# Selective scan of a fused Mamba-2 decoder layer: rows of cumulated time steps spread over the partitions by DMA instead of by TensorE

## What is computed

```python
zxbcdt = x @ w_in.T                       # z 512, xs 128, B 128, C 512, dt 4
xBC = silu(causal_conv4(xBC) + conv_b)
dt = softplus(dt + dt_bias); a = dt * -exp(A_log)
cs = cumsum(a, axis=time)                 # per sequence and head
Ldec = where(t >= s, exp(cs[t] - cs[s]), 0)
att = (C @ B.T) * Ldec
Y = att @ (xs * dt) + D * xs
y = Y * silu(z); out = y @ w_out.T
```

## Time and profile before

| | |
|---|---|
| median of 3 runs | 413.46 us |
| span of the profiled execution, first to last instruction | 411.9 us |
| the profiled execution's own time | not listed apart; the span is 1.6 us under the median |
| TensorE busy | 398.4 us, 97% of the span, 1936 matmuls |
| VectorE busy | 288.8 us, 70% |
| ScalarE busy | 189.7 us, 46% |
| POOL busy | 130.2 us, 32% |
| chain that ended last | TensorE 82%, VectorE 11%, ScalarE 3% |
| DMA | 25.52 MB in 11659 packets |

### The profile page before, as it was taken

The page is one execution under the profiler, slowest core; times in us unless marked ns, Lnnn a source line. Parts: engine busy times, 40 slices in busy tenths (PEclk is TensorE's granted clock), DMA queues, the critical chain, the costliest instruction groups (busy, mean ns, idle before and its releaser), DMA issues.

```text
span 411.9 us, 5385 instructions
## 1 busy us (share of the span) xinstructions
PE 398.4 (97%) x1936; PEld 318.3 (77%) x1936; DVE 288.8 (70%) x517; ACT 189.7 (46%) x383; POOL 130.2 (32%) x117
## 2 busy tenths in 40 slices
PE   7999999999999989999999999999999999999984
PEld 3878887766669987888888888887788788787753
DVE  3596991146886669888897989695567656675676
ACT  6768745736555564343425252863314133142131
POOL 3504215614524553565654737740000000000000
PEclk8999999999999999999999999999999999999999
DMA  7901111010000106111112131352110120110002
GB/s 248 316 2 52 53 51 51 2 51 2 0 1 2 52 2 204 53 51 53 51 51 60 44 99 49 113 179 74 51 53 25 52 78 25 51 54 22 28 0 77
DMA packets 11659, 25.52 MB, mean 62 GB/s; under 512 B 1681, under 2 KB 1809, under 8 KB 11634
## 3 DMA queue, kind: packets, MB, share of 16 engines
q1 hardware_dynamic: 10482, 23.10, 17.1%
q10 hardware_dynamic: 1152, 2.10, 1.4%
HBM read 23.10 MB, written 2.10 MB: 61 GB/s over the span
## 4 chain that ended last, share of the span: by engine, by line
PE 82%; DVE 11%; ACT 3%; issue 1%; DMA 1%; SPq 0%; ACTq 0%; DVEq 0%
PE bank L582 23%; PE bank L584 23%; PE bank L583 23%; PE bank L653 2%; PE bank L640 2%; PE bank L847 2%; PE bank L858 1%; DVE sets_f L1491 1%; DMA rows<-x 1%; PE bank L869 1%; PE bank L621 1%; DVE tmp L1668 1%; PE bank L662 1%; DVE big L1459 1%; PE bank L829 1%
## 5 line engine op out<-in xcount | busy, mean ns | idle before, releaser
L582 PE MATMUL bank<-sets,station 128*128 128x512 f32 (+1 forms) x424 | 164.1, 387 | 1.8 <-DVE station L1539 1.2
L584 PE MATMUL bank<-sets,station 128*128 128x512 f32 (+1 forms) x424 | 158.5, 374 | 0.0
L583 PE MATMUL bank<-sets,station 128*128 128x512 f32 (+1 forms) x424 | 158.3, 373 | 0.0
L582 PEld LDWEIGHTS bank<-sets,station 128*128 128x128 f32 x424 | 80.0, 189 | 19.5 <-issue 3.6
L583 PEld LDWEIGHTS bank<-sets,station 128*128 128x128 f32 x424 | 79.9, 189 | 15.4 <-issue 2.2
L584 PEld LDWEIGHTS bank<-sets,station 128*128 128x128 f32 x424 | 79.8, 188 | 14.3
L540 POOL TENSOR_TENSOR big<-tmp,side_f 128x512 f32<-128x512 f32 x17 | 26.4, 1569 | 24.0 <-DVE side_f L1555 24.0
L1425 DVE SCALAR_TENSOR_TENSOR big<-bank,cw,big 128x508 f32<-128x508 f32 (+2 forms) x36 | 26.2, 739 | 5.1 <-ACT big L1026 4.2
L462 POOL TENSOR_TENSOR station<-raw,station 128x1024 fp32r<-128x1024 f32 x7 | 16.8, 2395 | 40.2 <-ACT station L968 40.2
L1269 ACT ACTIVATE small<-small 128x1 f32<-128x1 f32 x24 | 7.0, 294 | 47.9 <-DVE small L1670 47.9
L1555 DVE TENSOR_TENSOR side_f<-side_f,bank 128x512 f32<-128x512 f32 x36 | 24.5, 684 | 4.1 <-PE bank L584 3.8
(11 more groups left out here) (182 smaller groups left out, 670.8 us busy)
## 6 DMA issues: line engine op xcount, KB each, us to landing
raw<-wstream SPq DMA_DIRECT2D x31, 512.0 KB, 3.4
rows<-x SPq DMA_DIRECT2D x8, 256.0 KB, 5.0
big<-ctxT SPq DMA_DIRECT2D x8, 256.0 KB, 2.6
big<-ctx SPq DMA_DIRECT2D x8, 256.0 KB, 2.9
out<-tmp ACTq DMA_DIRECT2D x8, 256.0 KB, 2.0
big<-ln_w SPq DMA_DIRECT2D x1, 256.0 KB, 5.4
big<-lora_b SPq DMA_DIRECT2D x3, 64.0 KB, 5.2
ga<-gate_lora SPq DMA_DIRECT2D x1, 72.0 KB, 5.3
```

Source lines behind the costliest of these rows:

```text
L582: pe.matmul(ps, a_hi, b_lo, start=first, stop=False)
L583: pe.matmul(ps, a_hi, b_hi, start=False, stop=False)
L584: return pe.matmul(ps, a_lo, b_hi, start=False, stop=last)
```

## The change

Row h of the running sums is copied by DMA from its one partition to all 128, four DMAs of 256 KB for each half (`spread_decays`), into `decays`, which holds 4 heads x 512 tokens a half. VectorE adds the mask once for each half (`mask_decays`), ScalarE takes the exponential in place, and att, skip and y_of work on that buffer. The five matmuls (L638, L640) go. The dt rows are computed twice, in partitions 0 to 3 and 32 to 35, with a multiplier of 1 for the second set, so that one 128x128 turn of `steps` gives both columns. time_steps of both halves moves up to behind conv_taps(3). The first half's buffer is in the memory of set T2, which is written again by the turned tiles later.

```diff
-N_TAPS = 4
-DT_LO = 32
+N_TAPS = 5
+DT_ROW = 32
+DT_LO = 2 * DT_ROW
+STEP_ROWS = DT_ROW + H
...
-        dec = big[:, 10752:11776].rearrange("p (b h q) -> p b h q", b=2, h=H)
-        negcs = big[0:H, 11776:12800]
...
+        decays = (at("decays0", SETS_AT + T2 * 2 * CH, [P, 2 * CH])[:, :], big[:, 10752:12800])
...
+        future = big[:, 13056:13184]
...
-        dt_row = tmp[0:H, 2048:3072]
-        sel = tmp[0:H, 3072:3584].rearrange("p (h q) -> p h q", h=H)
+        steps = tmp[:, 2048:3072]
+        negcs = steps[0:STEP_ROWS, :]
+        dt_row = sets[0:STEP_ROWS, T3, 0, :, :].rearrange("p c n -> p (c n)")
...
+        def dec(b):
+
+            return decays[b // HB].rearrange("p (h t) -> p h t", h=H)[:, :, bass.ts(b % HB, L)]
...
-            for dst, src in ((alog[:, :], a_log), (dtb[:, :], dt_bias), (cw[:, :, :], conv_w), (cb[:, :], conv_b)):
+            sp.wait_ge(small_set, 1)
+            for dst, src in ((alog, a_log), (dtb[0:H, :], dt_bias), (dtb[DT_ROW:STEP_ROWS, :], dt_bias),
+                             (cw[:, :, :], conv_w), (cb[:, :], conv_b)):
...
+            def spread_decays(hf):
+
+                sp.wait_ge(cs_ok, HB * (hf + 1))
+                for h in range(H):
+                    sp.dma_start(decays[hf][:, bass.ts(h, HALF)],
+                                 steps[h:h + 1, half(hf)].unsqueeze(1).broadcast_to([1, P, HALF])) \
+                        .then_inc(decays_in[hf], 16)
+
             for n in range(RAW, LOOP_CHUNK):
                 sp.wait_ge(w_lo, n - RAW + 1)
                 load_chunk(n)
+                if n == RAW + 2:
+                    spread_decays(0)
+                    spread_decays(1)
...
+            pool.memset(steps, 0.0).then_inc(pool_setup, 1)
...
+                    w_dt, lo_dt = blocks(ringS[:, 0, 0, 0:D]), blocks(ringS[:, 0, 1, 0:D])
+                    pool.tensor_copy(w_dt[:, :, DT_LO:DT_LO + H], lo_dt[:, :, 0:H].bitcast(F32)).then_inc(dt_lo, 1)
+                    pool.tensor_copy(w_dt[:, :, DT_LO + DT_ROW:DT_LO + STEP_ROWS], lo_dt[:, :, 0:H].bitcast(F32)) \
+                        .then_inc(dt_lo, 1)
+                    pool.tensor_copy(w_dt[:, :, DT_ROW:STEP_ROWS], w_dt[:, :, 0:H].bitcast(F32)).then_inc(dt_lo, 1)
...
                 pe.wait_ge(cs_ok, b + 1)
-                if b >= 2:
-                    pe.wait_ge(dec_exp, H * (b - 1))
-                if b == 0:
-                    pe.wait_ge(pool_setup, 8)
-                pe.matmul(bank[b % 2][:, :], identb[:, :], future, start=True, stop=False)
-                for h in range(H):
-                    pe.matmul(bank[b % 2][:, bass.ts(h, L)], sel[:, h, :], negcs[:, tok(b)],
-                              start=False, stop=(h == H - 1))
...
-                pe.transpose(bank[5][:, P:P + H], negcs[:, tok(b)], ident[0:H, 0:H])
-                pe.transpose(bank[5][:, P + H:P + 2 * H], dt_row[:, tok(b)], ident[0:H, 0:H])
+                pe.transpose(bank[5][:, P:2 * P], steps[:, tok(b)], ident[:, :])
...
-                act.activation(xb[:, b % 2, :], bank[5][:, 0:P + 2 * H], ACT.Copy).then_inc(xb_ok, 1)
+                act.activation(xb[:, b % 2, :], bank[5][:, 0:P + STEP_ROWS], ACT.Copy).then_inc(xb_ok, 1)
                 act.wait_ge(xb_ok, b + 1)
+                act.wait_ge(masked, b // HB + 1)
                 for h in range(H):
 
-                    act.activation(dec[:, b % 2, h, :], bank[b % 2][:, bass.ts(h, L)], ACT.Exp,
+                    act.activation(dec(b)[:, h, :], dec(b)[:, h, :], ACT.Exp,
...
+            v.memset(small[0:STEP_ROWS, 2:5], 1.0).then_inc(small_set, 1)
...
-                if i == 4:
+                if i == 3:
                     softplus_relu(1)
-            time_steps(0)
-            v.wait_ge(pool_setup, 8)
+                    time_steps(0)
+                    time_steps(1)
+
+            def mask_decays(hf):
+
+                d = decays[hf].rearrange("p (k q) -> p k q", q=L)
+                v.wait_ge(decays_in[hf], 16 * H)
+                v.tensor_tensor(d, d, future.unsqueeze(1).broadcast_to([P, HB * H, L]), ALU.add).then_inc(masked, 1)
+
+            v.wait_ge(pool_setup, 6)
+            mask_decays(0)
             v.wait_ge(const_in, 16 * N_CONST)
             for h in range(H):
                 mm = v.tensor_scalar(dI[:, h, :], ident[:, :], dsk[:, h:h + 1], None, ALU.mult)
             mm.then_inc(vec_setup, 1)
-            time_steps(1)
+            mask_decays(1)
```

More of the change, by code:

```diff
@@ L222, in build @@
         dsk = small[:, 5:5 + H]
-        dtb = small[0:H, 2:3]
+        dtb = small[0:STEP_ROWS, 2:3]
         alog = small[0:H, 3:4]
-        expa = small[0:H, 4:5]
+        expa = small[0:STEP_ROWS, 4:5]
         ga = sb("ga", [P, DC, E + E * RANK])
@@ L262, in build @@
         dt_ok, a_ok, cs_ok = sem("dt_ok"), sem("a_ok"), sem("cs_ok")
+        small_set = sem("small_set")
+        decays_in = [sem(f"decays_in{i}") for i in range(2)]
+        masked = sem("masked")
         cv_init, cv_tap, cv_done = sem("cv_init"), sem("cv_tap"), sem("cv_done")
@@ L444, in _ @@
             pool.memset(ident[:, :], 0.0).then_inc(pool_setup, 1)
-            pool.memset(sel, 1.0).then_inc(pool_setup, 1)
+            pool.memset(future, 0.0).then_inc(pool_setup, 1)
             pool.wait_ge(pool_setup, 2)
@@ L448, in _ @@
                                base=0, pattern=[[-1, P]], channel_multiplier=1).then_inc(pool_setup, 1)
[L449 to L453, removed]
             pool.affine_select(out=future, in_=future, compare_op=ALU.is_ge, fill=FUTURE, base=0,
-                               pattern=[[0, H], [1, L]], channel_multiplier=-1).then_inc(pool_setup, 1)
+                               pattern=[[1, L]], channel_multiplier=-1).then_inc(pool_setup, 1)
+            pool.memset(steps, 0.0).then_inc(pool_setup, 1)
             for e in range(E):
@@ L661, in y_of @@
                     pe.wait_ge(z_done, 6)
-                pe.matmul(bank[7][:, :], xb[:, b % 2, 0:P], dec[:, b % 2, :, :], start=True, stop=True) \
+                pe.matmul(bank[7][:, :], xb[:, b % 2, 0:P], dec(b), start=True, stop=True) \
                     .then_inc(y_ps, 1)
@@ L1006, in softplus_rest @@
                 act.wait_ge(ip_done, n + 1)
-                act.activation(dt_row[:, half(hf)], bank[IN_BANK[n]][DT_LO:DT_LO + H, :], ACT.Copy).then_inc(sp_rest, 1)
+                act.activation(dt_row[:, half(hf)], bank[IN_BANK[n]][DT_LO:DT_LO + STEP_ROWS, :], ACT.Copy) \
+                    .then_inc(sp_rest, 1)
             def softplus_abs(hf):
@@ L1392, in softplus_sum @@
                 v.wait_ge(sp_rest, hf + 1)
-                v.tensor_tensor(dt_row[:, half(hf)], bank[IN_BANK[n]][0:H, :], dt_row[:, half(hf)], ALU.add) \
+                v.tensor_tensor(dt_row[:, half(hf)], bank[IN_BANK[n]][0:STEP_ROWS, :], dt_row[:, half(hf)], ALU.add) \
                     .then_inc(sp_sum, 1)
@@ L1457, in att @@
                 for h in range(H):
[L1459 to L1461 removed]
+                    v.scalar_tensor_tensor(out=dec(b)[:, h, :], in0=bank[6][:, bass.ts(h, L)],
+                                           scalar=xb[:, b % 2, P + DT_ROW + h:P + DT_ROW + h + 1],
+                                           in1=dec(b)[:, h, :], op0=ALU.mult, op1=ALU.mult).then_inc(att_ok, 1)
             def gate_y(b):
```

25 lines of the change are left out of this document (9 added, 16 removed).

## The result

The changed kernel took 460.76 us, the median of 4 runs (460.22 to 462.54), beside 413.50 us for the kernel before (4 runs, 413.33 to 414.28). The ratio is 1.1138, 95% interval 1.1116 to 1.1160: slower by 47.3 us. The forecast was 407.0; what happened is rival 1, which had 463, and the sign that the prediction named for being wrong is there: TensorE waits at tile 1's product for VectorE, whose mask waits for a DMA.

The account below looks back on a forecast made before the run. The prediction took TensorE, busy 68.5 of 69 us, to bound the scan, with VectorE and ScalarE cutting the gain: of 11.0 us removed 6.5 remain, other parts cost nothing, so 413.46 - 6.5 = 407.0 us; range 404 to 466.

Parts of the forecast that it names:

- rival 1: Spread DMAs: rows leave their partition one at a time, tile 1's product 51.3 us late; 463 us, chance 0.27.
- the sign that the prediction named for being wrong: At tile 1's product: TensorE waits for VectorE, whose mask waits for a DMA; no size given.
- Part 4: The eight 256 KB DMAs from one SBUF row each: landed by 47 us, needed by about 66.8 us.
- its two ends: Time of the eight DMAs: 5.2 us at 401 GB/s, or 83.6 us at one engine's 25.1 GB/s.
- Part 3: POOL, start and SP's queue: extra casts, memset and loads cost nothing, at most 0.3 us; no load starts later.
- Part 1: TensorE in the scan: 1.38 us less per tile, 11.0 for eight, of which 6.5 us reaches the end.
- some 0.03 us: Chain of tiles 0 to 4: added cost each of the larger xb copy and the exponential reading SBUF.
- The sum of 6.5 us: Scan: gain of 6.20 by tile 4's scores, some 0.6 more behind att(4), 0.3 taken off for small additions.
- the forecast's own case: Whole kernel: fast DMAs and part of TensorE's gain kept, 407.0 us, own range 402.4 to 411, chance 0.50.
- Part 2: VectorE: time_steps moved behind conv_taps(3) cost nothing, at worst 1 us; two masks of 2.3 us each are hidden.
- The sentence that warned of POOL for the masks: VectorE's masks: beside a reading POOL a small operation went from 0.41 to 1.49 us, but POOL is free then.
- the two slower rivals: Spread DMAs: one row at a time, 463 us, chance 0.27; two streams at a time, 421 us, chance 0.15.

Follow-up runs that it names:

- Experiment 1: Kernel before plus extra 256 KB DMAs into unused memory, single, then paired on two queues; one SBUF row to 128 partitions landed in 11.0 to 11.3 us.
- experiment 4: Changed kernel with the second half's mask moved on VectorE from ahead of att(0) to ahead of att(4): 460.31 us, one run.
- experiment 2: Changed kernel with the eight DMAs copying each partition's own row and a constant exponential bias, decays left out of the result: 408.19 us, ratio 0.9856.
- experiment 5: Changed kernel with each half's four rows written to HBM first and spread from there: 409.57 us, ratio 0.9881.
- experiment 7: Rows by way of HBM, plus empty matmuls in TensorE's waits at tile 5's product and the turn of tile 3: 407.19 us; also tried on two other versions.
- the fill: 10 and 12 empty 256-column matmuls in TensorE's two 2 us waits, added to the version by way of HBM: 407.19 us against 409.57 without.
- experiment 6: Kernel before with only time_steps of both halves moved behind conv_taps(3): 414.86 us, ratio 1.0024; other places were tried in the version by way of HBM.
- kernel of taps(4): Version by way of HBM with time_steps of both halves behind conv_taps(4) instead of conv_taps(3): 413.38 us, ratio 0.9977.

## Why the prediction was wrong, point by point

**The step that failed is Part 4's choice between its two ends.** Both ends were worked out, 5.2 us of DMA and 83.6, and I took the lower one, because the load of ln2_w "has the same packets and destination". It has; but its source is in HBM, and the disputed thing was the source. Of the three properties in which that row could match (packets, destination, source) it matched the two that were not in question. Experiment 1 separates them: 3.1 us from HBM, 11.2 from one SBUF partition, 2.3 from 128. The upper end took one engine's pace, 25.1 GB/s, for copies that leave one at a time; measured were 27.3, a first issue at 38.7 us and a landing at 117.3 (forecast of that rival: 37.3 and 120.9). In place of 5.2 us and a landing by 47 us stand 78.6 us. That the 16 engines are busy for 0.91 of the time meanwhile rules out that a single engine does all the copies; that its pace was close to the measured one is luck, as far as the runs show.

The Trainium skill, "SBUF — State Buffer", section "Door 1: The DMA port swizzle", gives about 27 GB/s to a port and puts partitions 0 to 3 on one. The measured 27.3 GB/s agrees with the figure. The estimate made from it, about 456 us in all, was 5 us off; the prediction set it aside because no row tested it for reads. The same page of the Trainium skill, section "Can I just issue two DMAs to hit both halves?", says that two concurrent DMAs, one at partition 0 and one at 64, serialize, with only 6% more bandwidth than one. The pairs of experiment 1 agree in the main (18.9 us with partition 64, where one behind the other would be 22.6 and side by side 11.3). The table of ports under "Door 1: The DMA port swizzle" in the Trainium skill puts 0, 1 and 32 on one port, 4 and 64 on others. The ends of the pairs agree (21.1 and 20.7 us against 18.6 and 18.9); the landing of SP's copy does not (21.1 with 1, but 11.7 with 32).

**Rival 1 was right in its places too.** It had the second mask done at 123.2, att(0) done behind it and tile 1's product 51.3 us late, 1.7 us for the clock and 3.7 gained back later; measured 119.6, 47.7 us, 1.7 and 3.5 by the turn of tile 3. Part 3 missed one thing that would have cost as much by itself: "SP's queue ... no load starts later. Its data, though, lands behind theirs" takes an issue to be short. Once some copies are under way, an issue takes 9.59 us, so chunk 7, ready at 44.3, was issued at 94.9 and landed at 118.6; ScalarE's high part of it holds decay(1) (experiment 4). Its deadline was not in the sum. The last four spreads and this chunk are held by the same slow source, so this is a second path of one cause.

**Part 1, TensorE, was right in its mechanism, and can be read in experiments 2, 5 and 7.** A 128x128 turn takes 0.11 us from start to start and not 0.25, so a tile loses 1.66 us rather than 1.38:

```profile
64.02 0.27 PE L659 MATMUL bank<-ident,big 128*128 128x128 f32 x1
64.13 0.27 PE L660 MATMUL bank<-ident,tmp 128*128 128x128 f32 x1
64.24 1.02 PE L663 MATMUL bank<-big 128*128 128x512 f32 x2
```

The error cost nothing. On the other side the four exponentials of a tile take 1.28 us from SBUF and took 1.14 from the bank; "some 0.03 us" rested on no row. The wait ahead of out_proj(0) was forecast at 0.70 and is 0.6; that of tile 5's product at 1.4 and is 2.0; that before the turn of tile 3 was named and is 2.0. The sum of 6.5 us for the whole is what experiment 7's kernel has where TensorE's clock is full throughout: y_of(7) starts at 114.86 instead of 121.28, 6.4 us earlier, and its span is 405.3 (forecast 405.4). That it fits so well is luck in part: the conv stage gives back 1.0 us that the sum had at nothing, so that tile 1's product is 2.3 us earlier and not 2.76, and the shorter turns make up for it by tile 4 (6.6 us, forecast 6.20). Experiment 2, without the fill, has 4.6 us there. What was missing in the forecast's own case was the price of the waits that the gain turns into: 1.6 us of half clock behind the wait at the turn of tile 3. The earlier trace rows had shown the clock at half, and I charged it to the rival with 50 us of idle time alone.

**Part 2, VectorE: no cost, "at worst 1 us"; it is 1.0** (experiment 6). The sum had taps(4) 1.5 us later and 0.8 us of room behind that. In after they start 3.3 us later against taps(3) (41.05 and 31.61 us, before 37.87 and 31.71), because beside POOL the first time_steps takes 3.8 us, where I had 2.51 from its old place, and softplus_relu 1.0, where I had 0.4. That is 1.0 us more than the room, and the wait is 0.94. The sentence that warned of POOL for the masks was not applied to the steps. The masks took 2.29 us each as forecast (2.3), and with fast rows they were hidden. **The rest of Part 3**, the casts, the memset and the small loads at the start, cost nothing that any run shows.

**The chances.** 0.27 for rival 1 was too little on what the profile bore out, and the 0.43 for slower is 0.01 more than the two slower rivals hold together. The one row for the lower end did not test the claim, and the end above had a mechanism. The range, 404 to 466, held the result because it covered both.

## What to carry to other kernels

Before taking a price from "the nearest row", list in what the new operation differs from it, and ask whether the row tests that one thing; if it does not, the row is no evidence between the ends. To spread one row of SBUF over the partitions by DMA, write it to HBM first and spread it from there: here 1.6 to 3.3 us for the write and 3.6 us (median) from issue to landing for each of four copies under way together, instead of 9.6 us for each copy. And when work taken off a full TensorE turns into waits, count what each wait does to the granted clock, and look at what else stands on the queue that issues the new transfers.

## What the runs showed of the hardware that was not expected

- One SBUF row as the source of 128 copies of 2 KB landed 11.0 to 11.3 us after its issue, whichever partition it lay in (0, 5, 64); several in a queue went at 27.3 GB/s, with the 16 DMA engines recorded busy at a share of 0.91.
- Two such spreads at a time took 18.6 and 18.9 us from partitions 0 and 4 or 64, 20.7 and 21.1 from 0 and 32 or 1, so a second source partition helps little.
- SP's issues of such spreads took 0.6 us for the first two, 6.8 for the third and 9.6 us for each of the other five, and everything behind them on the queue waited.
- A 128x128 turn behind another costs TensorE 0.11 us from start to start.
- Beside POOL VectorE's four running sums of 4x128 took 3.52 us (kernel of taps(4)), alone 1.36; a `tensor_scalar` of 512 columns 1.00 and 0.47; the mask of 2048 columns 3.61 and 2.29.
- ScalarE's four exponentials of 128x128 took 1.28 us with SBUF as the source and 1.14 with a bank.
- A wait of 2.04 us before the turn of tile 3 cost TensorE 1.6 us more by the clock, and twelve empty matmuls in it won that back; a wait of 1.97 us at tile 5's product left the clock at 1.00 in experiments 2 and 5 and lowered it in after.
